# One semaphore for four gathers, column loads behind the mask, and VectorE's gathered work spread over a slot, in a one-core graph kernel

## The reference

```python
h = relu(layernorm(x))
H = gelu(h @ W1.T + b1)
X_src = H[src]
W_tar = gelu(X_src @ WA.T) @ WB.T                    # 4 mix weights of an edge
agg = gelu(segment_sum(X_src[:, :, None] * W_tar[:, None, :], dst))
out_edge = einsum('ehm,em->eh', agg[dst], W_tar)
agg_node = segment_sum(out_edge, dst) / max(segment_sum(1, dst), 1)[:, None]
out = x + gelu(concat([agg_node, H])) @ W2.T + b2
```

## Time and profile before

| | |
|---|---|
| median of 3 runs | 1404.87 us (1402.53 to 1408.35) |
| profiled execution: time | 1403.32 us |
| profiled execution: span, first to last instruction | 1401.6 us |
| mean granted clock of TensorE | 0.900 of full |
| instructions | 25933 |
| DMA | 203.93 MB, mean 146 GB/s |
| stage 0 | about 90 to 288 us |
| stages 1 to 4 | to about 473, 694, 920 and 1152 us |
| stage 5 and the epilogue | to 1342 and 1402 us |

### The profile page before, as it was taken

The page is one execution under the profiler, slowest core; times in us unless marked ns, Lnnn a source line. Parts: engine busy times, 40 slices in busy tenths (PEclk is TensorE's granted clock), DMA queues, the critical chain, the costliest instruction groups (busy, mean ns, idle before and its releaser), DMA issues.

```text
span 1401.6 us, 25933 instructions
## 1 busy us (share of the span) xinstructions
PE 1102.8 (79%) x7372; PEld 741.7 (53%) x7381; DVE 880.6 (63%) x2541; ACT 646.5 (46%) x1472; POOL 806.3 (58%) x879
## 2 busy tenths in 40 slices
PE   5945776768897898788878888777877778788987
PEld 3723433446565665556646655555555555455644
DVE  8546777736675477677547777747776756253266
ACT  6965666624333265545336555636555632000022
POOL 5455656556555665645656556665555656666335
PEclk9977978889999999989989989989999999899978
DMA  6444555555554644444545545454544546686533
GB/s 208 133 119 145 157 172 159 172 172 160 163 152 144 172 136 141 125 121 132 143 138 140 136 131 143 126 156 135 138 122 111 138 133 184 170 194 192 175 50 83
DMA packets 99537, 203.93 MB, mean 146 GB/s; under 512 B 29074, under 2 KB 48096, under 8 KB 98731
## 3 DMA queue, kind: packets, MB, share of 16 engines
q1 hardware_dynamic: 74948, 147.46, 34.7%
q0 software_dynamic: 24448, 54.81, 16.1%
HBM read 169.71 MB, written 32.48 MB: 144 GB/s over the span
## 4 chain that ended last, share of the span: by engine, by line
PE 54%; issue 13%; DVE 13%; ACT 7%; another core or an unknown queue 6%; DVEq 5%; DMA 2%; POOL 1%; ACTq 0%; SPq 0%; POOLq 0%
PE ps L1639 26%; PE ps L1605 11%; PE ps L1574 10%; DVE big L1221 4%; DVE q L1230 3%; DVEq L1176 2%; PE ps L1644 2%; PE ps L1578 2%; ACT hot_b L906 2%; PE ps L1591 2%; DVE big L1208 2%; ACT big L833 1%; DMA q<-product_parts 1%; DMA out_dram<-q 1%
## 5 line engine op out<-in xcount | busy, mean ns | idle before, releaser
L790 POOL DMA_INDIRECT q<-node_table,src_g x764 | 736.2, 964 | 498.6 <-issue 183.1
L1639 PE MATMUL ps<-big,q 128*128 128x316 bf16 (+1 forms) x2940 | 584.7, 321 | 42.6 <-issue 28.1
L906 ACT ACTIVATE hot_b<-iota_b,q 128x128 bf16<-128x128 bf16 x882 | 280.8, 389 | 406.4 <-PE ps L1605 251.6
L1639 PEld LDWEIGHTS ps<-big,q 128*128 128x128 bf16 x2940 | 277.2, 102 | 184.8 <-issue 60.9
L1221 DVE TENSOR_TENSOR big<-big,ps 128x294 f32 (+2 forms) x441 | 244.3, 554 | 198.4 <-PE ps L1605 100.2
L1605 PE MATMUL ps<-q,hot_b 128*128 128x294 bf16 (+2 forms) x882 | 221.6, 336 | 183.2 <-DVE big L1221 105.9
L1230 DVE TENSOR_SCALAR q<-iota_a,q 128x294 bf16<-128x294 f16 (+2 forms) x882 | 254.3, 330 | 45.1 <-issue 33.4
L1574 PEld LDWEIGHTS ps<-mask,q 128*128 128x128 f32 x1528 | 211.8, 208 | 34.2 <-issue 19.6
L1574 PE MATMUL ps<-mask,q 128*128 128x96 f32 x1528 | 216.1, 287 | 14.3 <-issue 10.3
L1605 PEld LDWEIGHTS ps<-q,hot_b 128*128 128x128 bf16 x882 | 85.8, 100 | 266.5 <-DVE big L1221 148.8
L1208 DVE TENSOR_TENSOR big<-big,ps 128x120 f32 x382 | 105.9, 277 | 151.1 <-PE ps L1578 56.2
(11 more groups left out here) (149 smaller groups left out, 674.6 us busy)
## 6 DMA issues: line engine op xcount, KB each, us to landing
q<-product_parts SPq DMA_DIRECT2D x245, 388.0 KB
product_parts<-big SPq DMA_DIRECT2D x24, 776.0 KB
q<-node_table,src_g POOLq DMA_INDIRECT x764
node_table<-big SPq DMA_DIRECT2D x12, 280.0 KB, 2.9
big<-node_table SPq DMA_DIRECT2D x24, 140.0 KB
own_part<-big SPq DMA_DIRECT2D x12, 256.0 KB, 3.0
out_dram<-q SPq DMA_DIRECT2D x11, 256.0 KB, 2.0
dense_columns<-q SPq DMA_DIRECT2D x4, 632.0 KB
```

The source lines that it names most:

```text
L790: pool.indirect_dma_start(out=ring[:, t % R, :], out_offset=None, in_=table, in_offset=bass.IndirectOffsetOnAxis(ap=src_g[:, t:t + 1], axi ...
L906: last = nc.scalar.activation(hot_b[:, b % 2, i, :], iota_b[:, :], ACT.Abs, bias=nkey_b[:, t:t + 1])
L1639: last = nc.tensor.matmul(ps[:, 3 + m, 0:n], cb[:, LEAD + P * (MIX * part + m):LEAD + P * (MIX * part + m + 1)], counts[k % 2][:, a, c0:c1 ...
```

## The change

It does three things. The four gathers of a pair count on one semaphore, and the mask waits for that one at 64 a lap (the same in the path for general inputs, which these inputs don't take). In `prepare_gathers` the `column` loads come after the mask instruction. And `make_eq` and the two `add_group` of a slot are dealt out: one `add_group` ahead of each count, one `make_eq` behind it, and what is left behind the last count.

```diff
+PT = 2 * G
-        gathered = [sem(f"gathered{i}") for i in range(R)]
+        gathered = [sem(f"gathered{i}") for i in range(R // PT)]
...
-                ).then_inc(gathered[t % R], 16)
+                ).then_inc(gathered[t % R // PT], 16)
...
             def make_masks(g):
                 s = G * g % R
-                for t in range(2 * G):
-                    v.wait_ge(gathered[s + t], 16 * (G * g // R + 1))
+                v.wait_ge(gathered[s // PT], 16 * PT * (G * g // R + 1))
...
             def prepare_gathers(slot):
                 for g in slot.gathers:
-                    starts_g[g] = column(regs_g[g % 8], base_g[:, g:g + 1], N - D0)
                     if g % 2 == 0:
                         make_masks(g)
                         if g + 2 < NG:
-                            make_eq(g + 2)
+                            due_eq.append(g + 2)
+                for g in slot.gathers:
+                    starts_g[g] = column(regs_g[g % 8], base_g[:, g:g + 1], N - D0)
...
-                while len(pending_g) >= 2:
-                    add_group(pending_g.pop(0))
-                    add_group(pending_g.pop(0))
-                pending_g += slot.gathers
+                due_g = pending_g[:len(pending_g) // 2 * 2]
+                pending_g = pending_g[len(due_g):] + slot.gathers
                 for c in slot.counts:
+                    if due_g:
+                        add_group(due_g.pop(0))
                     prepare_counts(c.number + AHEAD)
                     add_counts(c)
+                    if due_eq:
+                        make_eq(due_eq.pop(0))
+                for g in due_g:
+                    add_group(g)
+                while due_eq:
+                    make_eq(due_eq.pop(0))
```

More of the change, by code:

```diff
@@ L815, in step @@
                                 in_offset=bass.IndirectOffsetOnAxis(ap=idx[:, s:s + 1], axis=0),
-                            ).then_inc(gathered[s], 16)
+                            ).then_inc(gathered[s // PT], 16)
                 general_path(pool, step)
@@ L1330, in _ @@
             make_eq(0)
-            pending_g = []
+            pending_g, due_eq = [], []
             prepare_gathers(SLOTS[0])
@@ L1443, in _ @@
                                     ALU.is_equal).then_inc(eq_ready, 1)
-                                for t in range(G):
-                                    s = G * j + t
-                                    v.wait_ge(gathered[s], 16 * n + 16 * len(range(s, TG, R)) + 16)
+                                if j % 2 == 0:
+                                    i0 = G * j // PT
+                                    v.wait_ge(gathered[i0], 16 * PT * (n + 1 + len(range(PT * i0, TG, R))))
                                 v.wait_ge(eq_ready, GPS * n + NG + j + 1)
```

## The result

The changed kernel takes 1422.73 us (median of 4 runs, 1411.83 to 1424.90) beside 1403.70 us for the kernel before (4 runs, 1400.84 to 1408.35). The ratio is 1.0146, 95% interval 1.0105 to 1.0188: slower by 1.5%, outside the predicted range. Its profiled execution took 1424.9 us with a span of 1423.2.

A forecast was written before the change was run, and what follows sets the result against it. No engine is full; handing over between them bounds the kernel. 24 x 0.65 = 16 us, less 5 for a new wait, is 11, with a little from stage 0 12: 1403.3 - 12 = 1391 us, range 1374 to 1396.

The forecast's parts named there:

- The two take turns in waiting, over a double buffer: At the counts, TensorE waits 105.9 us for VectorE's adds and VectorE 185.0 us for TensorE's counts.
- Part one: One semaphore a pair ahead of the mask: removes about 10 us of VectorE queue time, nothing by itself.
- the first rival: The steady beat of GpSimd's gathers holds the time, floor 191 x 6.2 = 1184 us: no change, 1400 to 1404; chance 0.25.
- Part two, the loads: Column loads behind the mask: 29.4 us of queue gap in front of it go, 23 us come back.
- the 23 us said to come back in front of a slot's first add: New gap in 76 slots of stages 0 to 4 with two loads, 0.3 us each (7 to 40 us).
- Part three, the spreading: Second group add behind a count's add: 37.1 us of gap in front of it close, 24 us come back.
- The 24 us said to come back in front of line 1230: Gap before the one-hot tiles, the next count's load having short cover: 160 pairs x 0.15 us (none to 34).
- the net 20: VectorE's own sum: -29.4 - 37.1 + 23 + 24 = about -20 us, between -59 and +8.
- From VectorE's time to the kernel's: First counts served 0.65 us sooner; one in three of TensorE's 73 waits shrinks, 16 us, less 5 for a new wait.
- The late second add: Second group add and eq stand behind VectorE's wait for the first count: 14 us lost, about 1417; chance 0.15.
- the 10 us that I had named as a sign of being wrong: A wait of `sum_pair` for a group's add of more than 10 us would show the forecast wrong.
- That the beat isn't fixed: Sign to be read from a gain over 30 us; GpSimd's pairs of gathers start 6.16 and 6.36 us apart.

The follow-up runs named there:

- sem_only: The kernel before with only the change to one semaphore for a pair's four gathers: 1395.28 us, ratio 1.0067.
- spare_sems: The kernel before with five more semaphores allocated and never used: 1187.73 us, ratio 1.0011.
- after_again: The changed kernel, unedited, run again beside the kernel before at 1187.11 us: 1155.33 us, ratio 0.9728.
- spread_adds_only: The kernel before with only the group adds dealt out among the counts: 1392.47 us, ratio 1.0013.
- set 2: after_again, spare_sems and two other kernels, run on one chip beside the kernel before, which took 1187.11 us there.
- set 5: The changed kernel with 15 unused semaphores (1.0142) and with four semaphores a pair (1.0021), beside the kernel before at 1388.54 us.
- pool_on_added: The kernel before, with GpSimd's ring waiting for VectorE's adds instead of TensorE's group sums: 1589.73 us, ratio 1.1379.

## Why the prediction was wrong

**What bounds the kernel** was read rightly as handing over, but not what the handing over costs. "The two take turns in waiting, over a double buffer" took the 185.0 us of VectorE's wait for TensorE's work. Much of it, in this kind of set, is the delay of the report: an add that was waited for starts 2.47 us after its count has ended, where 0.15 to 0.27 us do in the other kind. The earlier trace rows had it in plain sight: the 1.4 to 1.7 us before each pair's first gather were put down to the pair's sum, which had ended 2.26 to 2.45 us before those three gathers, while the gathers before them still ran.

**Part one: "nothing by itself" is the step that failed.** With the rest of the change in place, the one semaphore costs 1.3% (1410.06 against 1391.39) and 1.9% (1421.67 against 1394.77), and alone 0.67%. The reasoning looked at queues and at the mask's wait; both are as it said (one semaphore instruction fewer a pair, 33.1 us instead of 44.3 in front of the mask in sem_only, no mask waiting longer). The price arises elsewhere, and its way is open. Without this part the change is flat in such sets: 0.9964 and 1.0021, the number of the first rival, "the beat holds it"; the fixed beat that it rests on isn't what the runs show (below).

**Part two, the loads**: the gap in front of the mask went from 44.3 to 1.0 us; I had left stage 5's 14.9 out, but they went too. Of the 23 us said to come back in front of a slot's first add a part did, hidden in a row that fell as a whole, 21.8 to 14.7. Put by its place in the slot, the "issue" idle in front of first adds in slots of stages 0 to 4 with two loads went from 0.4 to 7.3 us, and in the second kind of set from nothing in spare_sems to 11.8 in after_again. Over the 76 such slots 11.8 us are 0.16 us each, between the 0.09 and 0.53 of the forecast, which took 0.3. Where VectorE is waiting for reports anyway, such a gap hides.

**Part three, the spreading**: of the 43.8 us in front of group adds 22.8 are left, more than stage 5's 6.7. Stage 5 now has 8.8 of them, and of the 10.8 us of "issue" in stages 0 to 4, 10.0 stand in front of first adds, which are part two's; in front of second adds about 4 us are left there, so that gap closed as forecast. The 24 us said to come back in front of line 1230 did not come: 33.4 fell to 25.2. The gaps of the four places together went from 121.5 to 49.0 us, 72 us instead of the net 20, beyond the better end of 59. The Trainium skill (VectorE: DVE Perf Modes, The DRAIN you can't avoid) found no extra cost of a semaphore after each of eight chained copies; these short adds don't bear that out. In spread_adds_only, where nothing but the adds moved, the wait of an add for the other fell from 22.0 to 7.4 us, "issue" in front of the adds from 21.8 to 9.8 and in front of line 1230 from 33.4 to 19.8, with the mask's unchanged (44.3 and 43.4); sem_only, of the same set and with the adds together, has 21.3, 25.6 and 31.4. So the gap was closed and came back in none of these places.

**From VectorE's time to the kernel's.** I let a third of TensorE's 73 waits shrink by 0.65 us, 16 us. This is the second step that failed. In the first comparison the sum of these waits did not fall (105.9 and 108.2 us): VectorE arrives sooner and waits for the report instead, 185.0 to 283.2. Even where the sum was lower in a set of the first kind, the time was not: in spread_adds_only it is 80.1 us (97.2 in sem_only of the same set), with VectorE's wait at 136.8 + 97.2 = 234.0 and a ratio of 1.0013. In the second kind of set the step is right and too small: 26 us off 73.3, with 32 in all.

**The late second add** (third rival) has its sign right, but is not the cause: `sum_pair`'s wait for a group's add is 9.2 us, 8 times, and with four semaphores the spreading stays and the change is flat in the first kind of set. In the second kind this wait is larger, 7.8 us in spare_sems and 16.4 in after_again, above the 10 us that I had named as a sign of being wrong, and the change gains all the same. **That the beat isn't fixed** is shown by the second kind of set, where pairs follow at 979 / 190 = 5.2 us, not 6.5; the 1184 us called a floor is none; the gathers' own 961 is.

## What to carry to other kernels

A wait that ends late is to be measured from the end of the work that it waits for; where VectorE started over 2 us after the record of that work, moving its instructions forward bought nothing here, and its wait grew. A counting scheme that no one has to wait for can still have a price: keep one semaphore for each transfer in flight unless a run shows that sharing is free, and time it apart from the rest of the change. The version to keep here is the change with four semaphores a pair: 0.2% slower to 0.4% faster in one kind of set, 2.6 to 2.8% faster in the other, where the full change gives +1.5% and -2.8%.

## What was unexpected of the hardware

- The same kernel takes 1389 to 1404 us (medians) in three sets and the first comparison, and 1187 in two, with nothing between, and each set stays of its kind over up to 22 runs of the kernel before. Instructions last as long (a gather 0.964 and 0.966 us, a count's add 554 and 552 ns); what differs is how soon other engines learn of TensorE's work. TensorE's granted clock goes with it (0.900, and 0.939 in spare_sems), but TensorE's busy time differs by 73 us only, of 216. The first kind's profile also holds far fewer records of semaphore updates, 9781 against 22897 in spare_sems. Whether it is the chip or a state that it is in can't be told for sure; but the results give chip number 0 both for set 2, of the second kind, and for set 5, of the first, so a chip's number alone doesn't tell the kind.
- In the first kind, GpSimd's gathers mostly come in fours (129 of 158 unbroken runs in the kernel before); in the second, up to 544 follow without a break. Which semaphore GpSimd waits for plays no part in the delay (pool_on_added). TensorE's reports are late in and just after such a run and prompt later on (3.17 and 0.15 us in the kernel after, 4.44 and 0.14 in pool_on_added), and the late adds that begin with no gather running tend to do so 1.1 to 1.4 us after the last one has ended (the middle half of them in the kernel after). So in this kind the gathers hold the reports back, as far as the placing in time can show it; by what way, and why not in the second kind, is open, and no kernel without gathers was run.
- Sharing one semaphore among four indirect transfers costs 1.3 to 1.9% in the first kind, with the rest of the change in place, and nothing that can be measured in the second (0.9728 and 0.9723; 0.9715 and 0.9740).
